# Key and query rests moved in front of the parts in a shared SBUF region, and ScalarE's wait for the last stores moved from unit 2 to unit 4

## What is computed

```python
t = _to_tokens(x)                       # 32 samples, 400 tokens, 32 channels
t = t + attn(_ln_t(t))
t = t + ffn(_ln_t(t))                   # ffn: y = sigmoid(wx_t + y @ Vt), a scan over 512 steps

def attn(inputs):
    Q = inputs @ rot @ Wq.T;  K = inputs @ ent @ Wk.T;  V = inputs @ Wv.T
    dist2 = q2[:, :, None] + k2[:, None, :] - 2.0 * qk
    scores = exp(-dist2)
    attn = softmax(scores, axis=-1)     # so two exponentials, one inside the other
    return attn @ V
```

## Time and profile before

| | us |
|---|---|
| three runs | 224.82, 224.94, 226.02 |
| median | 224.94 |
| the profiled execution's own time | 225.0 |
| its span, first to last instruction | 223.1 |
| TensorE busy in the span | 198.2 |
| ScalarE busy | 169.6 |
| VectorE busy | 161.1 |

### The profile page before, as it was taken

The page is one execution under the profiler, slowest core; times in us unless marked ns, Lnnn a source line. Parts: engine busy times, 40 slices in busy tenths (PEclk is TensorE's granted clock), DMA queues, the critical chain, the costliest instruction groups (busy, mean ns, idle before and its releaser), DMA issues. The chain is left out here.

```text
span 223.1 us, 3444 instructions
## 1 busy us (share of the span) xinstructions
PE 198.2 (89%) x1182; PEld 98.8 (44%) x1182; DVE 161.1 (72%) x294; ACT 169.6 (76%) x307; POOL 28.7 (13%) x44
## 2 busy tenths in 40 slices
PE   6976999999999969699799999999999998499960
PEld 6833646546546435223243343434343423276730
DVE  0449459999999944985876595959687794676980
ACT  4064599599799798979988989899999955465540
POOL 7000000370150080250001010101010000000000
PEclk9999999999999999969999999999999999889995
DMA  6940200295889494697805334260700000000016
GB/s 185 366 149 11 68 7 0 34 316 186 238 275 309 88 302 160 203 309 172 225 5 170 56 116 108 46 181 8 215 0 3 0 0 0 1 1 3 0 53 244
DMA packets 26885, 26.87 MB, mean 120 GB/s; under 512 B 1550, under 2 KB 25806, under 8 KB 26740
## 3 DMA queue, kind: packets, MB, share of 16 engines
q1 hardware_dynamic: 26868, 26.64, 40.3%
HBM read 14.74 MB, written 11.88 MB: 119 GB/s over the span
## 5 line engine op out<-in xcount | busy, mean ns | idle before, releaser
L510 ACT ACTIVATE arena<-ps 128x800 f32<-128x800 f32 (+1 forms) x56 | 44.4, 795 | 6.4 <-PE ps L1066 4.3
L517 ACT ACTIVATE arena<-arena 128x800 f32<-128x800 f32 (+1 forms) x56 | 46.3, 828 | 0.0
L1066 PE MATMUL ps<-qa,ka 128*128 128x400 bf16 (+1 forms) x128 | 35.5, 341 | 2.9 <-ACT arena L510 2.3
L1066 PE MATMUL ps<-qb,kb 96*128 96x400 bf16 (+1 forms) x128 | 35.3, 338 | 0.0
L742 DVE TENSOR_TENSOR psum<-arena 128x400 f32<-128x400 f32 x32 | 19.6, 611 | 13.4 <-ACT arena L517 13.4
L742 DVE TENSOR_TENSOR psum<-psum,arena 128x400 f32<-128x400 f32 x32 | 19.5, 609 | 7.7 <-ACT arena L517 6.3
L1066 PEld LDWEIGHTS ps<-qa,ka 128*128 128x128 bf16 (+1 forms) x128 | 10.4, 97 | 26.8 <-ACT arena L510 13.2
L1099 PE MATMUL ps<-arena,vb 128*32 128x400 f32 x192 | 21.6, 525 | 0.8 <-issue 0.7
L751 DVE RECIPROCAL arena<-ps 128x400 f32<-128x400 f32 x7 | 18.5, 2649 | 0.0
L661 DVE COPY arena<-arena 32x400 f32<-32x400 f32 x48 | 17.2, 358 | 0.9
L587 ACT ACTIVATE yb<-ps 128x160 f32<-128x160 f32 x36 | 10.9, 304 | 8.0 <-PE ps L1183 6.7
(11 more groups left out here) (148 smaller groups left out, 360.4 us busy)
## 6 DMA issues: line engine op xcount, KB each, us to landing
dka<-arena SPq DMA_DIRECT2D x16, 200.0 KB, 2.6
dqa<-arena SPq DMA_DIRECT2D x16, 200.0 KB, 2.5
ka<-dka SPq DMA_DIRECT2D x8, 400.0 KB
qa<-dqa SPq DMA_DIRECT2D x8, 400.0 KB
arena<-x_tok SPq DMA_DIRECT2D x4, 400.0 KB
t<-x SPq DMA_DIRECT2D x1, 1600.0 KB, 11.4
dkb<-arena SPq DMA_DIRECT2D x8, 200.0 KB, 2.7
dqb<-arena SPq DMA_DIRECT2D x8, 200.0 KB, 2.7
```

The source lines that it names most:

```text
L510: nc.scalar.activation(prob[par][:, lo:hi, :], ps[:, o:o + hi - lo, 0:N], ACT.Exp, scale=2.0).then_inc(e1_done, 1)
L517: nc.scalar.activation(p, p, ACT.Exp).then_inc(p_ready, 1)
L1066: last = mm_(ps[row:row + keys, bank, 0:N], kk[par][0:rows, b, o:o + keys], qq[par][0:rows, b, :], start=first, stop=not first, skip_group ...
```

## The change

Two edits. The rests `rk` and `rq` are cut from the region ahead of the parts `kp` and `qp` instead of behind them. And ScalarE's wait for the stores of all parts goes from ahead of unit 2 of group 1 to ahead of unit 4; ahead of unit 2 stands a wait for the last parts having been made.

```diff
         rstd = [piece(N) for _ in range(2)]
         xl = [piece(N) for _ in range(2)]
+        rk = [piece(N) for _ in range(2)]
+        rq = [piece(N) for _ in range(2)]
         kp, qp = ([piece(3 * N // 2, BF16).rearrange("p (s n) -> p s n", n=N) for _ in range(2)]
                   for _ in range(2))
-        rk = [piece(N) for _ in range(2)]
-        rq = [piece(N) for _ in range(2)]
         es = piece(N)
...
                 for u in range(UNITS):
                     if since == 1 and u == 2:
+                        act.wait_ge(parts_ready, 2 * G)
+                    if since == 1 and u == 4:
                         for h in range(2):
                             act.wait_ge(kq_stored[h], 96 * PAIRS + CREDIT_DMA)
                     inner(g, par, u)
```

## The result

| | before | after |
|---|---|---|
| median of 17 runs, us | 224.98 | 223.74 |
| lowest | 223.84 | 222.30 |
| ratio of the times, 95% interval | | 0.9929 (0.9902 to 0.9956) |
| profiled execution: own time, span | 225.0, 223.1 | 223.46, 221.7 |

The change makes the kernel faster by 0.7%, 1.6 us by the ratio (0.99 to 2.2 by its interval), and 1.24 by the medians. The ratio leaves out the few executions in a slower state, the medians hold all 17. The forecast was 0.6 us: the measured time lies in the range of 223.6 to 225.1, but the gain is clear of noise and about twice the forecast or more.

What follows compares the result with a forecast made beforehand. TensorE, busy 89% of the span, was taken to bound the kernel. Group 1's first products 0.60 us earlier, new places at nothing, gave 225.0 - 0.6 = 224.4 us (224.3 against the median); range 223.6 to 225.1.

Steps and rivals of the forecast that it cites:

- no cost of the moved wait at unit 4: Group 1, ScalarE: it comes to the moved wait after 102.3, the stores having landed at 100.2, so nothing is lost.
- none of the new places: Rests' new places: no instruction added, reads and writes the same in size and number, so put at nothing.
- everything behind B at the same distances: After the first products of group 1, TensorE has no gap; everything from group 3 on comes 0.6 us earlier.
- The gap at 108.05: TensorE's 0.73 us idle before the first products of group 1, said to wait for VectorE's quotient; shrinks to about 0.15.
- that rival: The gap before group 1's first products has another cause than the quotient; nothing moves, 225.0 us; chance 0.13.
- The meeting with GpSimd: VectorE's add, moved earlier, meets GpSimd's instruction of 106.04 to 106.49 and ends at 106.92 rather than 106.60.
- the term that stood for no meeting: Without VectorE meeting GpSimd, group 1's first products start at 107.97, gaining 0.81 us, the upper end; lower end nothing.
- The clock falls elsewhere, to the good: Rival: the tail escapes TensorE's clock fall ahead of the recurrence, gaining up to 0.8 us more, 223.6; chance 0.10.
- the gate at 106.51: Group 2's first scores wait for a small operand load issued by SyncE, independent of ScalarE; they start at 106.51 again.
- unit 2's scores end at 99.15: Group 1: unit 2's last score matmul starts at 98.82, takes 0.33; ScalarE's exponential then starts at 99.19, 1.04 earlier.
- all of 1.65 us arrives: Rival: ScalarE's whole wait is gained because group 2's operands land earlier or the gate fails; 223.35 us; chance 0.04.
- The slower rival: Rival: the low clock begins only with the recurrence's first step, losing 1.6 and regaining 0.8; 225.2 us; chance 0.06.

Runs made afterwards that it cites:

- the kernel with the places alone: Changed kernel with ScalarE's wait for the stores left ahead of unit 2 of group 1, only the rests moved: 225.15 us, ratio 1.0019 to before.

## Why the prediction was right or wrong

**Right, step by step in the first profile:** ScalarE's exponential of unit 2 at 99.19 (99.27 measured), the outer one at 101.52 (101.54), the reciprocal at 103.52 (103.53), the first scores of group 2 at 106.51 (106.51), no cost of the moved wait at unit 4, none of the new places (shown by the kernel with the places alone), everything behind B at the same distances (B to S 84.19 and 84.21). The gap at 108.05 hung on the quotient, as argued from the code where the profile said "issue": that rival falls. In all eleven profiles in which TensorE stood idle ahead of B with no releaser named, B comes 0.09 to 0.10 behind the quotient's end.

**The meeting with GpSimd was on the wrong side.** The prediction let VectorE's add wait for GpSimd, for 0.32 us, and put B at 108.18. It was 107.98, the end of the term that stood for no meeting. VectorE's add began at 106.10 and GpSimd's instruction at 106.07; GpSimd's took 0.40 more and the two adds together 0.07. It was no accident of one execution: GpSimd's instruction took 0.85 or 0.86 in all six profiles of changed kernels with a fall in group 1. The Trainium skill (page "SBUF — State Buffer", section "Who interferes with whom") leaves it to the order of issue who stands still. The trace agrees that one of the two pays nearly all, but by the recorded starts the one that was first, by 0.03, is the one that paid, so these starts do not tell the order.

**The step that failed** is that the sum put the clock ahead of the recurrence at nothing and left it to a rival, "The clock falls elsewhere, to the good", with 0.8 us and a chance of 0.10. Its size was right (0.76), its place in the argument wrong. I held against it that the idle time before the recurrence keeps its length. It did, 2.81 before and after, and the fall stayed away in the first profile all the same: 225.0 - 0.71 - 0.76, less the 0.09 ahead of A, is the measured 223.46 within rounding. By the mean clock of the runs this is the common case (0.98 or more in 20 of 29 runs against 9 of 115 before), and 22 fillers that keep the clock in the kernel before gain it 1.0 us. So the term belonged in the sum. Why the shift keeps the clock is shown in part only, as said above.

**A second step was too small.** That the gate at 106.51 does not move, and that unit 2's scores end at 99.15, were read from one execution. The scores' end hangs on a clock fall in group 1, which came in some executions and not in others. Where it comes, the change is worth 0.5 to 0.9 in the attention stage (A to B 14.61 to 14.67 with the old wait, 13.78 to 14.08 with the new one); where it does not, 1.8 to 1.9 (14.67 and 14.77, against 12.86 once and 12.85 three times): all of the wait. The rival "all of 1.65 us arrives", 0.04, is what happened in the second profile of the changed kernel; its argument against, that SyncE's issues do not depend on ScalarE, was true and beside the point, since in these profiles the first scores of group 2 could start 10.7 to 11.4 behind A, not 12.3, though the last load was issued 5.5 to 6.2 behind A in these as in all others. What decides how early it lands stays open: the two kernels with ScalarE's wait at unit 2 in which the clock did not fall in group 1 and a load held the scores had it at 12.2 and 12.5.

**The slower rival** did not come: in neither series with it did the changed kernel lose. The second profile did lose the clock ahead of the recurrence, but no run shows a fall that begins only on the first step.

## What to carry to other kernels

A wait that ends 1.65 us late on one engine is worth on the bounding engine what its last dependent there was late, and this must be followed through the third engine: here TensorE lost to ScalarE's wait only through VectorE's quotient. A saving of well under a microsecond went together with a later clock fall staying away, so when a trace shows a fall behind the moved work, price the time with it and without it, and give both a fair chance. One profile is not enough for that: two of the same kernel had their falls in different places. The mean granted clock of many runs tells how much time was spent at the low clock, but not where. A few filler matmuls in an idle time kept the clock up behind it in every profile here, but they pay only where the engine that they speed up is the one that holds the chain.

## What the runs showed of the hardware that I had not expected

The mean granted clock followed a shift of under a microsecond half an execution ahead of the recurrence: 0.98 or more in 20 of 29 runs with the change, in 2 of 12 with 0.75 us of matmuls put back, in 0 of 12 with 1.5, while in their profiles the idle time of 2.81 us directly ahead of the recurrence was the same. The Trainium skill (page "TensorE: Matmul & The Clock Gate", section "Part 1: The HAM clock gate (the "warmup" mystery)") says that what watches TensorE's activity runs free and does not start anew with the kernel; that the start of a fall is not set by the idle time alone agrees with these runs. Two profiles of the kernel before had their falls in different places (at 95.0 and 194.0, and at 17.7 and 191.8), which agrees too. By that alone the place might be a matter of chance from run to run; in part it was not, for in four profiles the second fall began 99.0 behind the first.

An instruction of GpSimd that took 0.45 us took 0.85 beside two adds of VectorE, which lost 0.07 together, and 0.85 or 0.86 in all six profiles in which they met so.
